# Fused cross-attention and quantized feed-forward on one core: norm sums of q from one f32 square, a cast moved to ScalarE, and large buffers at multiples of 512 bytes

## The reference, cut to what matters

```python
def xattn(hidden, enc, Wq, Wk, Wv, Wo, gq, gk):       # hidden [16,128,256], enc [16,128,128]
    q = rmsnorm((hidden @ Wq) per head, gq)           # 16 heads of 128
    k = rmsnorm((enc @ Wk) per head, gk)
    v = (enc @ Wv) per head
    attn = softmax(q k^T / sqrt(128))
    return (attn v) @ Wo
x = x + xattn(layernorm(x), ctx_1024, Wq, Wk, Wv, Wo, gq, gk)
x = x + ffn(layernorm(x), w_gate, w_up, w_down, ln_weight)
```

## Time and profile before

| What | us |
|---|---|
| Median of 3 runs | 479.24 (478.85 to 480.3) |
| The profiled execution, its own time | 480.16 |
| Its span in the profile | 478.3 |
| PE busy | 415.7 (87%) |
| DVE busy | 430.5 (90%) |
| ACT busy | 430.7 (90%) |
| POOL busy | 387.9 (81%) |

### The profile page before, as it was taken

One profiled execution on the slowest core, in us unless ns is written; L12 is line 12 of the kernel. 1 busy time (PEld: TensorE's weight loads), 2 busy tenths in 40 slices (PEclk: granted clock), 3 DMA queues, 4 the chain that ended last, 5 costly groups with the idle time before them and its releaser, 6 DMA issues.

```text
span 478.3 us, 14736 instructions
## 1 busy us (share of the span) xinstructions
PE 415.7 (87%) x4554; PEld 317.7 (66%) x4554; DVE 430.5 (90%) x1249; ACT 430.7 (90%) x1454; POOL 387.9 (81%) x362
## 2 busy tenths in 40 slices
PE   0399866899999999999999999999999589788895
PEld 0288754677787777777777787777777355365563
DVE  2879899899999999999999999999998857999995
ACT  3379899999999999999999999999999569899993
POOL 2024958799999999999999999999998947888882
PEclk9999999999999999999999999999999989999999
DMA  7941734477465465555455465465666442001001
GB/s 270 427 183 24 287 65 83 61 114 144 89 118 100 88 119 100 96 111 101 89 113 105 92 117 98 90 119 99 98 103 108 94 78 34 1 33 35 22 33 58
DMA packets 140383, 50.20 MB, mean 105 GB/s; under 512 B 136000, under 2 KB 138048, under 8 KB 139456
## 3 DMA queue, kind: packets, MB, share of 16 engines
q1 hardware_dynamic: 139920, 48.78, 47.2%
q10 hardware_dynamic: 432, 1.05, 0.6%
HBM read 14.16 MB, written 2.10 MB: 34 GB/s over the span
## 4 chain that ended last, share of the span: by engine, by line
ACT 24%; issue 18%; POOL 17%; DVE 17%; DMA 10%; PE 9%; SPq 3%; ACTq 1%; POOLq 1%; DVEq 0%
ACT work L708 9%; DMA kT<-khl 8%; POOL rkq L553 5%; POOL phl L565 5%; PE SO L381 4%; ACT kjunk L746 3%; POOL work L543 3%; ACT qshl L730 3%; SPq L468 3%; ACT qhl L640 2%; ACT work L732 2%; DMA gqk<-in_gk 2%; PE KQ L381 2%; DVE ham L1245 2%; DVE qhl L1060 2%
## 5 line engine op out<-in xcount | busy, mean ns | idle before, releaser
L708 ACT ACTIVATE work<-SO,nbias,rkq 128x128 f32<-128x128 f32 x256 | 115.2, 477 | 6.0 <-DVE nbias L1083 4.5
L553 POOL TENSOR_TENSOR rkq<-kqe,negh 128x8 f32<-128x8 f32 x65 | 106.7, 1642 | 5.3 <-DVE kqe L1070 3.7
L381 PE MATMUL KQ<-hT,wqs 128*128 (+1 forms) x1536 | 99.4, 221 | 7.3 <-DVE wqs L932 6.7
L381 PEld LDWEIGHTS KQ<-hT,wqs 128*128 128x128 f16 x1536 | 92.0, 98 | 12.5 <-issue 10.0
L530 POOL TENSOR_TENSOR qshl<-work,qshl 128x512 f16<-128x512 f32 x64 | 74.5, 1163 | 27.1 <-ACT work L732 26.2
L381 PE MATMUL EB<-As,ohl 128*128 128x256 f16 x768 | 95.0, 274 | 0.4 <-issue 0.4
L381 PEld LDWEIGHTS EB<-As,ohl 128*128 128x128 f16 x768 | 75.5, 98 | 23.4 <-issue 1.4
L565 POOL TENSOR_TENSOR phl<-work,phl 128x512 f16<-128x512 f32 x64 | 74.0, 1156 | 19.7 <-DVE phl L1154 19.2
L381 PEld LDWEIGHTS SO<-kT,qhl 128*128 128x128 f16 x768 | 44.6, 98 | 37.0 <-DMA kT<-khl 22.4
L543 POOL TENSOR_TENSOR work<-work,rinv 128x512 f32<-128x512 f32 x64 | 66.6, 1040 | 3.0 <-DVE rinv L1028 2.9
L381 PE MATMUL SO<-kT,qhl 128*128 128x128 f16 x768 | 54.0, 220 | 12.1 <-DMA kT<-khl 8.0
(11 more groups left out here) (164 smaller groups left out, 930.5 us busy)
## 6 DMA issues: line engine op xcount, KB each, us to landing
xs<-in_xP SPq DMA_DIRECT2D x4, 512.0 KB, 22.2
stage<-in_wqP SPq DMA_DIRECT2D x4, 512.0 KB, 11.6
wvo<-in_woP SPq DMA_DIRECT2D x1, 2048.0 KB, 19.1
out<-wqs SPq DMA_DIRECT2D x16, 128.0 KB, 1.7
raw<-in_ctxT ACTq DMA_DIRECT2D x1, 1024.0 KB, 6.6
wvo<-in_wvP SPq DMA_DIRECT2D x1, 1024.0 KB, 14.7
raw<-in_ctxP SPq DMA_DIRECT2D x1, 1024.0 KB, 21.0
kT<-khl SPq DMA_TRANSPOSE x64, 3.1
```

The source lines that it names most:

```text
L381: last = matmul(out, lhsT=left(i), rhs=right(j), start=start and n == 0, stop=stop and n == 2)
L553: pool.tensor_tensor(rkq[:, g % 4, :], kqe[:, g % 2, :], negh[:, 0:2 * HG], ALU.pow).then_inc(root_ok, 1)
L708: ins = act.activation(pe[:, s, c], SB[:, c], ACT.Exp, scale=rkq[:, (g - AT_X + 1) % 4, HG + h:HG + h + 1], bias=nbias[:, s, h:h + 1], acc ...
```

## The change

- The norm sums of q are taken from the f32 squares directly: four f32 products with a column of f32 ones, in place of eight f16 ones. The f16 square on ACT, `q_square_low` on POOL, the buffer `qshl` and the semaphore `qslo_ok` go. `q_sums` waits for `qsq_ok`.
- In the loop's `step`, the cast of the probabilities to their f16 high half goes from DVE (between `residual` and `o_low`) to ACT (the last stage of the step, behind `o_high`). In `early` and `drain` it stays on DVE.
- `st6` is allocated first, and `khl`, `kT`, `qhl`, `phl`, `pT`, `ohl` directly behind the large buffers, so that all of these lie at multiples of 512 bytes.
- ACT issues the loads of gq and gk ahead of that of the context.

```diff
+        st6 = sb("st6", [P, B, 6])
         xs = sb("xs", [P, B, DM])
...
         wo_f = wvo[:, H * CD:6144].rearrange("p (h n) -> p h n", h=H)
+        khl = sb("khl", [P, 2, 2, GW], F16)
+        kT = sb("kT", [P, 2, 2, GW], F16)
+        qhl = sb("qhl", [P, 4, 2, GW], F16)
+        phl = sb("phl", [P, 2, 2, GW], F16)
+        pT = sb("pT", [P, 2, 2, GW], F16)
+        ohl = sb("ohl", [P, 2, 2, GW], F16)
         ident = sb("ident", [P, P], F16)
...
-        qshl = sb("qshl", [P, 2, 2, GW], F16)
...
-            def q_square_low(b, g):
-                if live(b, g, 0):
-                    s = g % 2
-                    need(pool, qsq_ok, b, g, 0)
-                    need(pool, ssq_ps, b, g, 0, 2)
-                    pool.tensor_tensor(qshl[:, s, 1, :], qsq[:, s, :], qshl[:, s, 0, :],
-                                       ALU.subtract).then_inc(qslo_ok, 1)
...
             def step(b, g):
-                q_square_low(b, g)
                 p_scaled(b, g)
                 kq_roots(b, g)
                 p_low(b, g)
...
-            act.dma_start(cT_f, ctxT).then_inc(cT_in, 16)
             act.dma_start(gqk[:, 0:1], gq).then_inc(g_in, 16)
             act.dma_start(gqk[:, 1:2], gk).then_inc(g_in, 16)
+            act.dma_start(cT_f, ctxT).then_inc(cT_in, 16)
...
                     need(act, ssq_ps, b, g, 0, 2)
-                    act.activation(qshl[:, s, 0, :], QB, ACT.Square, scale=SQ_SHIFT)
-                    need(act, qslo_ok, b, g, 0, 2)
                     act.activation(qsq[:, s, :], QB, ACT.Square, scale=SQ_SHIFT).then_inc(qsq_ok, 1)
...
+            def p_high(b, g):
+                if live(b, g, AT_X):
+                    s = (g - AT_X) % 2
+                    need(act, pn_ok, b, g, AT_X)
+                    need_dma(act, pT_in[s], b, g, AT_X, 2)
+                    act.activation(phl[:, s, 0, :], pn[:, s, :], ACT.Copy).then_inc(phi_ok, 1)
...
                 o_high(b, g)
+                p_high(b, g)
...
                 residual(b, g)
-                p_high(b, g)
                 o_low(b, g)
...
-                    need(te, qslo_ok, b, g, AT_SSQ)
+                    need(te, qsq_ok, b, g, AT_SSQ)
...
                     for h in range(HG):
-                        for a in range(2):
-                            ins = te.matmul(MB[:, h:h + 1], lhsT=qshl[:, s, a, h * P:(h + 1) * P],
-                                            rhs=ones[:, 0:1], start=a == 0, stop=a == 1)
+                        ins = te.matmul(MB[:, h:h + 1], lhsT=qsq[:, s, h * P:(h + 1) * P], rhs=ones_f[:, 0:1],
+                                        start=True, stop=True)
```

More of the change, by code:

```diff
@@ L106, in build_program @@
         gqk = sb("gqk", [P, 2])
-        st6 = sb("st6", [P, B, 6])
         mv = sb("mv", [P, B, 2])
@@ L132, in build_program @@
         rkq = sb("rkq", [P, 4, 2 * HG])
-        khl = sb("khl", [P, 2, 2, GW], F16)
-        kT = sb("kT", [P, 2, 2, GW], F16)
-        qhl = sb("qhl", [P, 4, 2, GW], F16)
         qsq = work[:, 2 * GW:4 * GW].rearrange("p (s n) -> p s n", s=2)
-        qshl = sb("qshl", [P, 2, 2, GW], F16)
         smax_sb = sb("smax", [P, 2, HG])
@@ L144, in build_program @@
         pss = sb("pss", [P, 2, HG])
-        phl = sb("phl", [P, 2, 2, GW], F16)
-        pT = sb("pT", [P, 2, 2, GW], F16)
         hf = work[:, 0:XB * DM].rearrange("p (s n) -> p s n", s=XB)
@@ L155, in hf_of @@
             return hf[:, b % XB, :]
-        ohl = sb("ohl", [P, 2, 2, GW], F16)
         KQ = pb("KQ", [P, 2 * GW])
@@ L228, in build_program @@
         qsq_ok = sem("qsq_ok")
-        qslo_ok = sem("qslo_ok")
         ssq_ps = sem("ssq_ps")
```

## The result

The kernel after takes 499.87 us (median of 4 runs, 496.69 to 500.16), the kernel before 479.05: a ratio of 1.0412 [1.0378, 1.0447]. The prediction was 495.0, between 487 and 505. The profiled execution of after took 499.66 us with a span of 497.4.

A forecast was written before the change was run, and what follows sets the result against it. PE was to become the bound: 54 x (5.49 - 5.14) = 18.7 us more, less 1.9, 0.5 and 0.5, gives +15.8 on the profiled 480.16, so 496.0; the median lies 0.9 lower, so 495, range 487 to 505.

The forecast's parts named there:

- The norm sums, 0.88 us: On PE, four f32 products make eight load records of 0.11 us: 0.88 us a step in place of 0.21.
- The rival that rested on the loads hiding (471 us): PE's norm sums take 0.21 to 0.44 us, ACT bounds, step about 5.03 us, total 471; chance 0.11.
- PE as the bound, 5.49 us a step, +18.7 us: In the loop, PE's step goes from 4.82 to 5.49 us and sets the pace: 18.7 us more over 54 steps.
- PE's share would rise to 92% or more: Sign in the profile after: PE's busy share goes up from 87% to 92% or more.
- The cast on ACT, 0.47 us from start to start, nothing gained or lost: In the loop, ACT loses a square and gains a cast, 0.47 us each, and stays at 4.82 us.
- added wait: The cast on ACT waits for POOL's scaled probabilities, which come earlier without POOL's square: costs nothing.
- POOL and DVE: gains that do not show: In the loop, POOL loses 1.11 us a step and DVE a 416 ns cast; PE covers both, so neither gain shows.
- The three-step cycle through kT: Loop from POOL's low half through transposes, scores and exponentials back: 16.0 us against 16.5 allowed, not binding by 0.5.
- Alignment, 0: New buffer placement could move transfers; with PE full put at 0, at most the 8.0 us PE idled behind kT.
- Order of the loads, 0.5 us gained: At the start, DVE waited 1.99 us for gk behind the context; loading it earlier gains 0 to 2.0, taken as 0.5.
- The early steps, 1.9 us gained: Before 90.65 us, some four ACT-led steps lose a square and gain no cast: 1.9 us gained, within 4 either way.
- The end: At the attention's end, PE's 1.43 us wait for POOL's low half goes and 0.67 of loads comes: 0.5 us gained.

The follow-up runs named there:

- Experiment 2: The kernel before with only the f32 norm sums (one f32 square, four f32 products, no low half on POOL); cast, loads and placement unchanged: 496.33 us.
- experiment 3: The changed kernel, context loaded ahead of gq and gk again, with one f16 square and four f16 products, low half left out of the norm sums: 474.41 us.
- 4: The changed kernel, context loaded first again, with square and ones in float32r and four products of two columns each: 478.48 us.
- experiment 7: The changed kernel, context loaded first again, with the four f32 norm products spread behind the three wide k products: 490.31 us.
- 8: The changed kernel, context loaded first again, with float32r norm products spread behind the wide k products and the cast back on DVE: 473.36 us.
- experiment 5: The kernel before with only the loop's cast of the probabilities moved from DVE to ACT, both squares kept: 513.81 us.
- experiment 6's counterpart: The changed kernel with the context loaded first again and the old placement of the buffers: 498.23 us.
- experiment 1: The changed kernel with only ACT's three loads in the old order again (context, then gq and gk): 497.51 us.

## Why the prediction was right, and where it was off

**The norm sums, 0.88 us.** Right: 0.86, from the 0.11 us between the two loads of one f32 product, times eight. Experiment 2 shows it alone; 3 and 4 show that it goes by the loads, their type and number, and not by the count of products: 0.10 us for four f16, 0.45 for four float32r, 0.86 for four f32. The Trainium skill, page "TensorE: Matmul & The Clock Gate", section "LDWEIGHTS (loading the stationary operand)", gives a load as its columns over 1.2, which is 107 ns for 128; the traces agree at 0.86/8 = 108 and 0.45/4 = 113 ns start to start, though a record lasts 192. The 25 ns for every product of up to 64 columns, in the same page's section "Back-to-back issue gap" of the Trainium skill, hold here for the f16 sums alone (0.10/4 and 0.21/8). The rival that rested on the loads hiding (471 us) is refuted as the kernel stands; in experiments 7 and 8 one load hid behind a wide product, and of two loads about one.

**PE as the bound, 5.49 us a step, +18.7 us.** Right: 5.478, +18.1. That PE's share would rise to 92% or more was wrong, it is 90% over the span: start and end dilute it, and in the loop it is 246.6 of 248.

**The cast on ACT, 0.47 us from start to start, nothing gained or lost.** Right for the whole change, if a little small: 0.52 to 0.54, and no wait. The reason given, that POOL has no square to do first, was the deciding one: without it the wait closes a ring of 5.7 us (experiment 5), and an "added wait" that shows as 0.2 us by its own row costs about half of the 34 us there.

**POOL and DVE: gains that do not show.** Right; 63 us less on POOL in the loop's stretch (234.1 to 171.1) moved nothing.

**The three-step cycle through kT, not binding by 0.5 us.** It did not bind in after. Its length itself was not measured.

**Alignment, 0.** Right for this change, by experiment 6's counterpart, for the reason given (PE is full). Alone it is worth 5.2 us (479.38, the kernel before beside it, less 474.14), within the bound of 8.0 that the prediction took from PE's waits for kT.

**Order of the loads, 0.5 us gained: the step that failed.** The prediction looked only at who gets its data sooner (`gg`) and noticed that it would not help, since Wq's block is next. It did not price the transfer that was moved behind the two: 1 MB issued 0.93 us later, landed 5.2 us later and held the first q product by 2.06. A term of -0.5 was +2.06.

**The early steps, 1.9 us gained.** Also wrong: +0.22. Steps 1 and 2 pay 0.66 and 0.64 us, the f32 loads in the open; experiment 3, without them, does these two in 5.66 and 7.52 where after needs 6.42 and 8.28. Step 4 gains 0.86 and step 7 0.36. Thus there are gains and losses of the right kind, but PE's part, taken as partly hidden, took all that ACT gave. **The end**, -0.5: measured -1.2.

Working in the profiled execution's time, the sum was 496.0 and the result 499.66. The 3.7 us are the load order 2.6 and the early steps 2.1, less 0.6 in the loop and 0.7 at the end, and 0.3 around the span. The loop was sized well, and the miss comes from ahead of it.

## What to carry to other kernels

Before replacing many narrow products by fewer of a wider type, count weight loads, not products: eight f16 loads behind each other were 0.21 us and eight f32 ones 0.86, and a wide product right ahead hid about one of the latter. An instruction moved to an engine that waits for POOL should be traced once round, from its own end back to its wait; an entry of 0.2 us a step in the list of waits can be the visible end of a ring that sets the step. And when DMA issues are reordered, price the transfer that goes back, in landing time, before the one that comes forward.

## What the runs showed of the hardware that was not expected

**A large transfer landed more than five times as late as it was issued late.** Issued 0.93 us later, the context landed 5.2 us later (10.8 us from issue to landing, 6.6 before). What SP's queue was loading came sooner in exchange: DVE's first instruction on x starts at 5.15 us in place of 6.99, ACT's first on Wk at 6.64 in place of 7.99. That SP's loads, issued ahead of the context now, took the DMA engines first is the likely cause, and was not tried apart.

**Placement moves DMA transposes.** 3.1 or 3.2 us to landing with the old addresses, 2.8 with buffers at multiples of 512 bytes, in both pairs of kernels. Only these two placements were run, so that 512 bytes is what matters is not shown.

**The clock fell ahead of the loop, in some executions.** Windows of experiment 1 (two lines), then of after:

```profile
74.00:78.00 4.00, 1.85 (x18) 1.62 (x17) 3.96 (x10) 3.65 (x13) 2.51 (x2) 0.92 0.58 131
78.00:84.00 6.00, 6.00 (x43) 5.17 (x41) 4.76 (x14) 4.97 (x13) 3.79 (x3) 0.50 0.43 92
```

```profile
78.00:84.00 6.00, 4.78 (x57) 4.30 (x58) 5.93 (x17) 5.64 (x23) 3.83 (x3) 1.00 0.31 71
```

In experiment 1's execution the granted clock was 0.50, that is 1.2 GHz, in this stretch, where after has 1.00, 2.4 GHz. Ahead of it PE had been busy only 1.85 of 4 us. That is no cause by itself: the kernel before has the same 1.85 us between 74 and 78, and its clock stays at 1.00 after them; what else it takes was not tried. The profiled executions of experiment 7 and of experiment 6's counterpart met the same stretch (0.50 between 78 and 84 us). Step 7 took 8.89 us in experiment 1 and 6.31 in after, and step 8 gave 0.3 back, so an execution can carry 2.3 us that have nothing to do with the edit. This is why the profiled executions of experiment 1 and of after lie only 0.8 us apart (498.84 and 499.66), where the start alone gives 2.0. The runs of experiment 1 spread over 4.6 us; whether such stretches make all of that spread was not looked at.
